# Feed-forward sums on TensorE: three float32 products a block become products of rounded parts and rests

## What is computed

```python
def shift_tokens(t):                      # the second half of the features comes from the token before
    a, s = jnp.split(t, 2, -1)
    s = jnp.pad(s, ((0, 0), (1, 0), (0, 0)))[:, :-1]
    return jnp.concatenate([a, s], -1)

def ffn_layer(x, g, bln, W1, b1, W2, b2):
    mu = x.mean(-1, keepdims=True)
    var = ((x - mu) ** 2).mean(-1, keepdims=True)
    xn = (x - mu) / jnp.sqrt(var + 1e-05) * g + bln
    hg = xn @ W1 + b1                     # 128 -> 2 x 341
    a, gate = jnp.split(hg, 2, -1)
    return a * jax.nn.gelu(gate, approximate=False) @ W2 + b2      # 341 -> 128
```

## Time and profile before

| what | before |
|---|---|
| median of 3 runs | 1655.81 us (1652.73 to 1659.36) |
| the profiled execution's own time | 1654.67 us |
| its span, first to last instruction | 1652.9 us |
| PE busy | 1566.3 us, 95% of the span |
| DVE, ACT, POOL busy | 1305.2, 1280.4, 1074.3 us |
| one slot in the middle (803.50 to 833.42 us) | 29.92 us |

### The profile page before, as it was taken

One profiled execution on the slowest core, in us unless ns is written; L12 is line 12 of the kernel. 1 busy time (PEld: TensorE's weight loads), 2 busy tenths in 40 slices (PEclk: granted clock), 3 DMA queues, 4 the chain that ended last, 5 costly groups with the idle time before them and its releaser, 6 DMA issues.

```text
span 1652.9 us, 89828 instructions
## 1 busy us (share of the span) xinstructions
PE 1566.3 (95%) x36944; PEld 1275.7 (77%) x36944; DVE 1305.2 (79%) x1944; ACT 1280.4 (77%) x2012; POOL 1074.3 (65%) x788
## 2 busy tenths in 40 slices
PE   7898699999999999999999999999999999999986
PEld 3575578888888888888888888888888888888865
DVE  5575778788887887888878888888788888887853
ACT  5796557788887888878888788788787887887853
POOL 2203767768767769667678676777776787767631
PEclk9899799999999999999999999999999999999989
DMA  3000224223324232333222342322343323232221
GB/s 128 2 0 1 55 68 113 63 60 75 92 56 113 71 74 65 79 106 82 61 64 69 95 111 57 71 71 65 85 110 75 71 53 91 71 76 63 60 69 34
DMA packets 75728, 116.75 MB, mean 71 GB/s; under 512 B 17294, under 2 KB 27276, under 8 KB 74764
## 3 DMA queue, kind: packets, MB, share of 16 engines
q1 hardware_dynamic: 75660, 115.99, 28.2%
HBM read 19.04 MB, written 1.05 MB: 12 GB/s over the span
## 4 chain that ended last, share of the span: by engine, by line
PE 90%; issue 4%; DVE 3%; ACT 2%; DVEq 0%; POOL 0%; DMA 0%; ACTq 0%; SPq 0%; POOLq 0%
PE ps L646 14%; PE ps L912 10%; PE ps L887 10%; PE ps L838 9%; PE ps L763 9%; PE ps L766 8%; PE ps L767 8%; PE ps L979 4%; PE ps L831 3%; PE ps L928 3%; PE ps L930 2%; PE ps L929 2%; PE ps L635 1%; DVE h L1648 1%; PE ps L919 1%
## 5 line engine op out<-in xcount | busy, mean ns | idle before, releaser
L448 POOL TENSOR_TENSOR arena<-arena 128x1024 f32<-128x1024 f32 x192 | 456.5, 2378 | 74.6 <-DVE arena L1578 60.9
L457 POOL TENSOR_TENSOR arena<-arena,rnorm 128x1024 f32<-128x1024 f32 x192 | 361.7, 1905 | 208.4 <-ACT rnorm L1189 208.3
L646 PE MATMUL ps<-cst,arena 64*128 64x64 f32 x6656 | 290.1, 230 | 27.1 <-issue 6.0
L646 PEld LDWEIGHTS ps<-cst,arena 64*128 64x128 f32 x6656 | 249.1, 140 | 84.8 <-issue 71.3
L1178 ACT ACTIVATE arena<-ps 128x1024 f32<-128x1024 f32 x192 | 196.8, 1025 | 100.7 <-DVE arena L1578 99.6
L1574 DVE TENSOR_TENSOR arena<-ps,rope 128x1024 f32<-128x1024 f32 x192 | 233.8, 1218 | 26.5 <-PE ps L767 26.5
L1578 DVE TENSOR_TENSOR arena<-ps,rope 128x1024 f32<-128x1024 f32 x192 | 233.3, 1215 | 0.0
L766 PE MATMUL ps<-wqkv_lo,x_hi 128*128 128x512 f32 x576 | 228.8, 397 | 0.0
L767 PE MATMUL ps<-wqkv_hi,x_hi 128*128 128x512 f32 x576 | 228.2, 396 | 0.0
L1588 DVE TENSOR_REDUCE norm<-arena 128x16 f32<-128x1024 f32 x192 | 224.5, 1210 | 0.3 <-ACT arena L1178 0.2
L763 PE MATMUL ps<-wqkv_hi,x_lo 128*128 128x512 f32 x576 | 201.4, 431 | 0.6 <-issue 0.6
(11 more groups left out here) (137 smaller groups left out, 2733.7 us busy)
## 6 DMA issues: line engine op xcount, KB each, us to landing
v_sb<-v_nat SPq DMA_DIRECT2D x576, 130.0 KB
v_sb<-v_nat SPq DMA_DIRECT2D x192, 65.0 KB
wqkv_sb<-wqkv SPq DMA_DIRECT2D x6, 1536.0 KB, 6.3
v_sb<-v_sb SPq DMA_DIRECT2D x96, 65.0 KB
wo_sb<-wo SPq DMA_DIRECT2D x6, 512.0 KB, 3.7
w_sb<-w SPq DMA_DIRECT2D x6, 341.0 KB, 4.0
x<-xT SPq DMA_DIRECT2D x1, 1024.0 KB, 4.8
scl<-scales SPq DMA_DIRECT2D x6, 128.0 KB, 6.1
```

What stands on the lines that cost most here:

```text
L448: pool.tensor_tensor(t_cos[:, m, j, :], t_cos[:, m, j, :], t_sin[:, j, :], ALU.add)\
L457: pool.tensor_tensor(x, x, rnorm[:, H * j:H * j + H].unsqueeze(2).to_broadcast([P, H, D]), ALU.mult).then_inc(s[done], 1)
L646: mm = pe.transpose(ps[0:width, bank + t, 64 * c:64 * c + 64], src[r], ident[r, r], tile_position=(64 * t, 0))
```

## The change

The three places where the feed-forward has a plain float32 product in a slot take the second way, and POOL makes the parts:

- **Mean and variance**: `mean_w` is rounded once to `mean_r`. POOL rounds `f_x` into `f_nh` and takes the rest `f_nl` (`part_x`), and later does the same with `f_sq` in the same two buffers (`part_square`). PE multiplies both by `mean_r`: two products in place of one float32 product.
- **Down-projection**: DVE writes the product of value and gate over the gate in `f_g`. POOL rounds all three tiles at once into `f_ah` and takes the rest `f_al` (`part_gated`, 768 columns). W2 is split once a layer (`split_down`, in the slot `after=3`). PE makes nine products in place of three.
- **The square** moves in ACT's queue from behind the table load to the place ahead of `copy_q`.
- The gates of pair f wait for `f_parted` of the pair before, since `f_g` is read by POOL. `f_a` is gone. The last three pairs, behind the last slot, keep the float32 products, and each has a buffer of its own for its gated values.
- The constants that only the start needs are loaded into the shared arena, in one more transfer; eight buffers more are set to zero at the start, DVE makes `mean_r` there, and two copies of the first attention's values (L531) come behind the wait for the roped keys.

```diff
+            def part_x(f):
+                pool.wait_ge(s["f_shifted"], CREDIT + 2 * f + 2)
+                pool.wait_ge(s["f_var"], CREDIT + f)
+                pool.sem_inc(s["pool_waited"], 1)
+                pool.tensor_copy(f_nh[:, :], f_x).then_inc(s["f_x_rounded"], 1)
+                pool.wait_ge(s["f_x_rounded"], CREDIT + f + 1)
+                pool.tensor_tensor(f_nl[:, :], f_x, f_nh[:, :].bitcast(F32), ALU.subtract)\
+                    .then_inc(s["f_x_parted"], 1)
...
+            def part_square(f):
+                pool.wait_ge(s["f_squared"], CREDIT + f + 1)
+                pool.wait_ge(s["f_mean"], CREDIT + f + 1)
...
+            def part_gated(f):
+                pool.wait_ge(s["f_prod"], CREDIT + 3 * f + 3)
+                pool.wait_ge(s["f_down"], CREDIT + f)
+                pool.sem_inc(s["pool_waited"], 1)
+                pool.tensor_copy(f_ah[:, :, :], f_g[:, :, :]).then_inc(s["f_rounded"], 1)
+                pool.wait_ge(s["f_rounded"], CREDIT + f + 1)
+                pool.tensor_tensor(f_al[:, :, :], f_g[:, :, :], f_ah[:, :, :].bitcast(F32), ALU.subtract)\
+                    .then_inc(s["f_parted"], 1)
...
-            def slot(g, norm=True, ahead=True, more=True, after=None, layer=None):
+            def slot(g, norm=True, ff=True, ahead=True, more=True, after=None, layer=None):
 
                 f = g - 2
                 scale(g, 1)
+                if norm:
+                    part_x(f)
                 if ahead:
                     rotate(g + 1, 0, 0)
                     low(g + 1, 1)
                     rotate(g + 1, 0, 1)
+                    if ff:
+                        part_gated(g - LAG)
+                    if norm:
+                        part_square(f)
+                    if after == 3:
+                        split_down(layer)
                     if after == 7:
                         table(layer, 1)
                         split_weights(layer, 2)
...
+            def mean_of_parts(parted, f, bank, done):
+
+
+                pe.wait_ge(s[parted], CREDIT + f + 1)
+                pe.matmul(ps[:, bank, 0:N], mean_r[:, :], f_nl[:, :], start=True, stop=False)
+                pe.matmul(ps[:, bank, 0:N], mean_r[:, :], f_nh[:, :], start=False, stop=True).then_inc(s[done], 1)
...
+            def down_parted(f):
+
+                pe.wait_ge(s["f_parted"], CREDIT + f + 1)
+                pe.wait_ge(s["w2_ready"], CREDIT + f + 1)
+                out = ps[:, 1, 0:N]
+                for i in range(3):
+                    r = slice(0, HT[i][1])
+                    high = f_ah[r, i, :]
+                    pe.matmul(out, w2_lo[r, i, :], high, start=(i == 0), stop=False)
+                    pe.matmul(out, w2_hi[r, i, :], f_al[r, i, :], start=False, stop=False)
+                    mm = pe.matmul(out, w2_hi[r, i, :], high, start=False, stop=(i == 2))
                 mm.then_inc(s["f_down"], 1)
...
                 if norm:
                     pe.wait_ge(s["f_gated"], CREDIT + 3 * (g - LAG) + 3)
-                    mean(g - 2, 6)
+                    mean_of_parts("f_x_parted", g - 2, 6, "f_mean")
...
                     if norm:
                         pe.wait_ge(s["centred"], CREDIT + 4 * g + 4)
-                        variance(g - 2, 2)
+                        mean_of_parts("f_sq_parted", g - 2, 2, "f_var")
...
-                        down(g - LAG)
+                        down_parted(g - LAG)
...
                 if ahead:
                     high(g + 1, 1)
                     square_of(g + 1, 0, 1)
+                if norm:
+                    square(g - 2)
                 copy_q(g, 1)
```

More of the change, by code:

```diff
@@ L156, in build @@
         o_t = take(12288, H // 2, N)
-        f_last = take(8192, 3, N)
+        f_last = {SLOTS - 3 + i: take(768 * i, 3, N) for i in range(3)}
         own = take(6144, 4, N)
@@ new lines, in split_down @@
+            def split_down(layer):
+                pool.wait_ge(s["w_2_loaded"], 32 * layer + 32)
+                pool.wait_ge(s["f_down"], CREDIT + B * layer)
+                pool.sem_inc(s["pool_waited"], 1)
+                for i in (0, 2):
+                    rows, w = (P, slice(0, 2)) if i == 0 else (HT[2][1], slice(2, 3))
+                    pool.tensor_copy(w2_hi[0:rows, w, :], w2_sb[0:rows, w, :]).then_inc(s["w2_high"], 1)
+                    pool.wait_ge(s["w2_high"], CREDIT + 2 * layer + 1 + i // 2)
+                    part = pool.tensor_tensor(w2_lo[0:rows, w, :], w2_sb[0:rows, w, :],
+                                              w2_hi[0:rows, w, :].bitcast(F32), ALU.subtract)
+                part.then_inc(s["w2_ready"], B)
@@ L560, in _ @@
             rotate(0, 1, 1)
-            slot(0, norm=False)
-            slot(1, norm=False)
-            slot(2, after=2, layer=0)
+            slot(0, norm=False, ff=False)
+            slot(1, norm=False, ff=False)
+            slot(2, ff=False, after=2, layer=0)
             with pool.Fori(0, DEPTH - 1) as layer:
                 first = pool.snap(layer * B)
-                with pool.Fori(LAG, 6) as b:
+                slot(pool.snap(first + LAG), after=3, layer=layer)
+                with pool.Fori(LAG + 1, 6) as b:
                     slot(pool.snap(first + b))
@@ L572, in _ @@
                 slot(pool.snap(first + 10), after=2, layer=layer + 1)
-            with pool.Fori(SLOTS - 5, SLOTS - 2) as g:
+            slot(SLOTS - 5, after=3, layer=DEPTH - 1)
+            with pool.Fori(SLOTS - 4, SLOTS - 2) as g:
                 slot(pool.snap(g))
@@ L1263, in round_norm, with gate @@
                 act.activation(f_hi[:, :], f_y, ACT.Copy).then_inc(s["f_high"], 1)
-            def gate(f, i, out, count):
+            def gate(f, i, out, count, last=False):
                 size = HT[i][1]
                 act.wait_ge(s["p_h_loaded"], 16 * layer_of(f) + 16)
-                act.wait_ge(s["f_prod"], CREDIT + 3 * f)
+                if not last:
+                    act.wait_ge(s["f_parted"], CREDIT + f)
+                elif f == SLOTS - 3:
+                    act.wait_ge(s["f_down"], CREDIT + f)
+                else:
+                    act.wait_ge(s["f_prod"], CREDIT + 3 * f)
                 act.wait_ge(s["f_gate_up"], CREDIT + 2 * f + count)
@@ L1318, in to_exps @@
                     round_weights(layer, 2)
-                if norm:
-                    square(g - 2)
                 if att:
@@ L1632, in subtract_mean, with product @@
                 dve.tensor_tensor(of[1], of[0], ps[:, bank, 0:N], ALU.subtract).then_inc(s["f_centred"], 1)
-            def product(f, i, value, count, gated=f_a):
+            def product(f, i, value, count, gated=f_g):
                 size = HT[i][1]
-                if gated is f_a:
-                    dve.wait_ge(s["f_down"], CREDIT + f)
                 dve.wait_ge(s["p_h_loaded"], 16 * layer_of(f) + 16)
@@ L1708, in _, with last @@
             slot(g, ahead=False)
-            def last(f, gated=f_a):
+            def last(f):
                 a, b, c = LAST_BANKS[f]
+                gated = f_last[f]
                 product(f, 2, ps[:, a, N:2 * N], 2, gated)
@@ L1731, in _ @@
             last(g - 1)
-            last(g, f_last)
+            last(g)
             add(g - 1, 7)
```

95 lines of the change are left out of this document (58 added, 37 removed).

## The result

The kernel of the change takes 1649.0 us (median of 7 runs, 1641.8 to 1654.5), the kernel before 1655.9 beside it (7 runs). The ratio is 0.9942, with a 95% interval of 0.9914 to 0.9969: faster by 0.6%. The two medians alone are 6.9 us apart, 0.4%. I had forecast 15 us, 0.9%. The profiled execution has 1644.68 us with a span of 1642.9.

What follows compares the result with a forecast made beforehand. PE was taken to bound the kernel, busy for 95% of the span. From 1654.67 us, 28 us of PE savings came off and 13 us of layer-change stalls were added: 1639.7, about 1640 us, range 1628 to 1664 us.

Steps and rivals of the forecast that it cites:

- faster: Whole kernel: an outcome below 1647.5 us, about 0.5% under the time before; chance 0.63.
- What PE saves: Mean and variance 0.19 us each, down-projection 0.25: 0.63 us a slot, 28 us over 45 slots.
- The rule of four passes: PE's products: true float32 takes four array passes, which would save 0.76 us a slot, 34 us in all.
- Can PE use it?: At the mean: the attend behind it also waits for copy_v, and the sooner mean fits by 0.2 us.
- Rival B: Gain eaten: layer changes cost 23 us (1650 us), or mean's 0.19 us lost to ACT (1649 us); chance 0.22.
- What POOL gets: POOL's new work: CAST at COPY's price; part_x and part_square 1.4 us each, part_gated 3.0 us.
- Rival A: Parts late at the variance in every slot if CAST costs a subtraction: 0.5 us a slot, 1681 us; chance 0.14.
- The ordinary slot: POOL finishes part_gated and part_square by 824.7, PE asks at 825.6: 0.9 us to spare, no stall.
- The change of layer: Five times, POOL works without a pause and PE stalls for it: 2.65 us each, 13 us in all.
- third stall: At a layer change: round_norm late, so copy_q and copy_k are late and the scores wait 0.5 us.
- The first stall: At a layer change: PE waits 1.7 us for POOL's parts at the mean.
- Start and end: Extra zeroing and the L531 copies lie off PE's path, the last three pairs keep their products: no cost.

Runs made afterwards that it cites:

- The run with three products: The kernel of the change with only three (hi*hi) of the nine down-projection products, so its output lacks the rest: 1645.1 us, ratio 0.9918.
- mean and variance alone: The kernel of the change with the down-projection back as three float32 products, without part_gated and split_down: 1649.2 us, ratio 0.9964.
- the down-projection alone: The kernel of the change with mean and variance back as float32 products: 1655.9 us, ratio 1.0002.
- the kernels with other orders: The kernel of the change with POOL work moved earlier at layer changes: rope table 1643.5 us; also part_x 1646.4; also part_square 1645.3.
- two of the moves: part_x and rope table early at layer changes; run on the kernel of the change with keys' transposes first and float32 down-projection: 1634.2 us, ratio 0.9879.
- the keys first alone: The kernel of the change with the keys' transposes, turn_k(g, 0), ahead of the queries', turn_q(g, 0): 1638.9 us, ratio 0.9885.

## Why the prediction was right, and where it was not

The time of 1649.0 lies in the range of 1628 to 1664, but above the 1647.5 us at which my chance of 0.63 for "faster" ended, in the part that had 0.22. The ratio of 0.9942 is past 0.5% by a little, that of the same kernel again, 0.9963, is not, and both intervals reach to either side: the times don't decide that question. The likeliest number, 1640, was 9 us too low.

**What PE saves** (right for PE, wrong for the slot). The products have the price forecast. Pieces of the chain at variance and down-projection, kernel after (start, us; answering to the earlier trace rows):

```profile
823.07 0.12 PE ps L997
823.20 0.12 PE ps L998
...
828.17 0.12 PE ps L1066
828.29 0.12 PE ps L1067
...
829.14 0.12 PE ps L1068
829.26 0.18 issue
```

Variance 0.24 for 0.43, and the down-projection 829.26 - 828.17 = 1.09 for 1.31. The row's 0.12 a product gave 1.06. The rule of four passes, which I set against the row (the Trainium skill, FP8 and Floating Point Precision, TensorE Precision Notes), gives an estimate of 0.98 us for the nine products, which is further off; a saving of 34 us was not to be had.

**"Can PE use it?"** This is the step that failed. I asked it of the mean alone, where the `attend` behind it had 0.2 us to spare. I took it for granted of the down-projection, "after which the next slot's `turn_q` begins". The rows of before already show who decides there; PE and ACT, kernel before:

```profile
801.16 1.46 PE L979 MATMUL ps<-f_a,w_sb 128*128 128x256 f32 x6
801.46 1.03 ACT L1211 ACTIVATE v_nat<-ps 128x1024 f32<-128x1024 f32 x1 [0.93 <-PE ps L767]
...
802.59 0.30 PE L646 MATMUL ps<-cst,arena 64*128 64x64 f32 x3
```

and the same place in the kernel after:

```profile
828.01 0.28 PE L1066 MATMUL ps<-f_ah,w_lo 128*128 128x256 f32 x1
...
828.30 1.04 ACT L1298 ACTIVATE v_nat<-ps 128x1024 f32<-128x1024 f32 x1 [0.77 <-PE ps L835]
...
828.98 0.28 PE L1068 MATMUL ps<-f_ah,w_hi 85*128 85x256 f32 x1
...
829.43 0.71 PE L714 MATMUL ps<-cst,arena 64*128 64x64 f32 x16 [0.18 <-issue]
```

Before, the copy of v ended at 801.46 + 1.03 = 802.49 and `turn_q` started at 802.59. After, 829.34 and 829.43. From the start of the down-projection to `turn_q` it is 1.43 us before and 1.42 after. The chain of before puts 1.31 us of that stretch down to L979, since PE was busy for it; but the copy ended at nearly the same time, and holds `turn_q` up just as long once the down-projection is shorter. The run with three products confirms it: 830.92 - 829.50 = 1.42 once more. What is left to the down-projection comes by the residual's add, which now ends sooner for the first `attend` of the slot. Both kernels with the float32 down-projection wait there (waits of PE, kernel before and mean and variance alone), and the kernel after and the down-projection alone have no such row:

```profile
PE ps L887 <- DVE h L1648: 8.7, 42, 0.3
```

```profile
PE ps L952 <- DVE h L1738: 8.1, 39, 0.3
```

From the start of `turn_q` to this `attend` it is 0.91 us (median of the slots read) in the two kernels with the float32 product and 0.74 in the two with parts: 0.17 us, close to the 0.15 that the down-projection is worth on top of the others. In the kernel with the down-projection alone 0.11 of it is lost again between the mean and `turn_q(g, 1)` (1.58 us for 1.47 before), which leaves its 0.08 within a few hundredths; what delays PE there was not tested.

The mean lost part of its gain too. `turn_q(g, 1)` waits for DVE's subtraction of the mean, which starts at the mean's end. Kernel after, PE and then DVE:

```profile
813.03 0.28 PE L997 MATMUL ps<-f_nl,mean_r 128*128 128x256 f32 x1
813.15 0.29 PE L998 MATMUL ps<-f_nh,mean_r 128*128 128x256 f32 x1
813.36 0.86 PE L955 MATMUL ps<-v_sb,arena 64*32 64x66 f32 x64
814.41 0.71 PE L714 MATMUL ps<-cst,arena 64*128 64x64 f32 x16 [0.18 <-issue]
```

```profile
813.73 0.42 DVE L1725 TENSOR_TENSOR f_a<-f_a,ps 128x256 f32<-128x256 f32 x1 [0.43 <-PE ps L998]
```

From the mean's start to the subtraction's start it is 0.70 us after, and 816.63 - 815.84 = 0.79 before: 0.09 saved of 0.19. From the mean's start to `turn_q(g, 1)` PE has the same 0.09 (1.47 us before, 1.38 after). With the variance's 0.19 (whose place in PE's order has no such follower) and some 0.15 of the down-projection that makes 0.43, the slot's gain. Rival B had this size, with the mean's 0.19 lost to ACT. Its number, 1649, was hit with a different loss: less of the mean's, and most of the down-projection's. The slot's missing 0.2 us, 45 times, is 9 us, the size of the miss. (The sum was built on the profiled execution, and that of the kernel after, at 1644.7, lies only 5 us above it: such single times scatter by as much.)

**What POOL gets** (right). CAST at the COPY's price, 0.40 and 0.826 us. Rival A, which needed a CAST as dear as a subtraction, is out. The best case of a tight loop (the Trainium skill, GPSIMD Engine Reference, Side-by-side cycle accounting), 1.8 cycles or 1.5 ns an element by that page, is not the floor for this instruction: the two casts give (826 - 399) / 512 = 0.83 ns an element. The same section of the Trainium skill has 1.03 cycles for the shortest loop bodies, by estimate 0.86 ns an element at 1.2 GHz, and the trace agrees with that.

**The ordinary slot** (right for POOL). No wait of PE for POOL's parts in any, and POOL stands idle for 0.41 us ahead of `scale(g+1, 0)`, where I had half a microsecond or less. Moving the square cost nothing and was not needed: put back, the slot is the same. My remark that without the move the square "would be ready for POOL only behind the table load" was true and without consequence.

**The change of layer** (right in sum, half wrong in its places). 5 x 2.4 us against 5 x 2.65. My third stall was too long even by my own figures: the scores are due later by the second stall too, which makes it 0.1 to 0.3 us in place of 0.5. And 46 slots less the first two are 44 and not 45, 0.6 us in all. PE and POOL at the mean, and DVE and PE behind it, kernel after (answering to the earlier trace rows):

```profile
872.67 0.72 POOL L522 TENSOR_TENSOR f_nl<-f_a,f_nh 128x256 fp32r<-128x256 f32 x1
...
883.02 0.74 POOL L482 TENSOR_TENSOR rope<-cst,scl 128x256 f32<-128x256 f32 x1
```

```profile
873.54 0.36 PE L997 MATMUL ps<-f_nl,mean_r 128*128 128x256 f32 x1 [1.23 <-POOL f_nl L522]
```

```profile
884.06 1.23 DVE L1667 TENSOR_TENSOR arena<-ps,rope 128x1024 f32<-128x1024 f32 x1 [1.53 <-POOL rope L482]
```

The first stall is the mean's, 1.23 us where I had 1.7. The variance, for which I had 0.45, doesn't wait. In its place the rope table, which `part_gated` and `part_square` push back, holds up DVE for 1.53 us, then ACT for 3.00 and PE for 0.64 at L831, behind the logarithm. I had followed the table's 0.7 us as a duration in POOL's queue and had not asked who waits for it. But fixing one or the other gives little: in the 30 us from 858 POOL is busy for 29.2. Most of the stall follows from POOL's load, as the kernels with other orders show, and the late instruction is only where it shows.

**Start and end** (right as far as can be seen). The first add stands at 293.61 before and 293.21 after; other runs differ by far more than that.

## What to carry to other kernels

A busy bottleneck engine's piece in the chain of waits is worth shortening only if what comes next on that engine waits for nothing else that ends at the same time. Look at the end of every other operation that the next instruction waits for, in the same rows: here a copy that ended 0.1 us before the successor's start made 0.25 us of saved work worth 0.08 to 0.15. Before work is handed to an engine with free time, find the one stage where that engine has none: there a better order mostly moved the wait, and leaving out the piece with the least return (here the down-projection's parts), together with two of the moves, gave the shortest sum of slots of the study (1269.5 us). By the times it can't be told from the keys first alone.

## What the runs showed of the hardware

- As forecast, but in no row of before: a CAST to `float32r` on POOL takes the COPY's time, and less than half of the two-input subtraction of the same 768 columns (0.826 against 1.821 us).
- A float32 product of 256 columns takes 0.43 us and a `float32r` product 0.12, so that three `float32r` products (0.36) are cheaper than one float32 by 0.07 us only; the large gain is where one factor needs no rest, as in the mean, with two products at 0.24.
- The usual slot and the changes of layer of one kernel repeat to 0.05 us in its two profiled executions, at a granted clock of 1.00, while one kernel's end differs by 3 us. The stretch ahead of the first add spans 7 us over all the kernels, at granted clocks of 0.89 to 0.93; the two executions of the same kernel have it equal (293.21 and 293.24). Two of the kernels with the keys first have the same 43 spacings in all (1274.0 and 1273.9 us), and medians that lie 4.5 us apart.
